# Attention inside a three-stage kernel: the key chunks of a half in two parts of four units instead of four parts of two

## What is computed

```python
q, k, v = (proj(Wq), proj(Wk), proj(Wv))
dots = jnp.einsum('bhqd,bhkd->bhqk', q, k) * scale
attn = jax.nn.softmax(dots, axis=-1)
out = jnp.einsum('bhqk,bhkd->bhqd', attn, v)
out = out.transpose(0, 2, 1, 3).reshape(b, n, INNER)
out = jnp.einsum('bne,ce->bnc', out, Wo)
return out + x
```

## Time and profile before

| | |
|---|---|
| median of 3 runs | 408.19 us (408.17 to 408.68) |
| profiled execution, its own time | 409.11 us |
| its span | 407.2 us |
| TensorE busy | 395.0 us, 97% |
| VectorE busy | 224.5 us, 55% |
| ScalarE busy | 254.7 us, 63% |
| GpSimd busy | 292.7 us, 72% |

### The profile page before, as it was taken

One profiled execution on the slowest core, in us unless ns is written; L12 is line 12 of the kernel. 1 busy time (PEld: TensorE's weight loads), 2 busy tenths in 40 slices (PEclk: granted clock), 3 DMA queues, 4 the chain that ended last, 5 costly groups with the idle time before them and its releaser, 6 DMA issues.

```text
span 407.2 us, 6494 instructions
## 1 busy us (share of the span) xinstructions
PE 395.0 (97%) x2518; PEld 238.1 (58%) x2518; DVE 224.5 (55%) x304; ACT 254.7 (63%) x347; POOL 292.7 (72%) x145
## 2 busy tenths in 40 slices
PE   8898999999999999999999999999999989999996
PEld 8765554454555445544645555464558535489995
DVE  1798765565656555656665565657563700564322
ACT  1556566676667575767676575858573596436763
POOL 3062088969899989999998999899989487900011
PEclk9999999999999999999999999999999999999999
DMA  7000101011220121012103222240125014000001
GB/s 247 2 1 0 54 0 54 6 47 26 82 52 2 54 54 52 3 54 54 52 2 105 48 110 54 54 150 7 57 52 157 0 55 155 2 1 14 15 26 53
DMA packets 28507, 20.49 MB, mean 50 GB/s; under 512 B 21276, under 2 KB 23708, under 8 KB 28476
## 3 DMA queue, kind: packets, MB, share of 16 engines
q1 hardware_dynamic: 27900, 19.09, 17.3%
q10 hardware_dynamic: 576, 0.98, 0.7%
HBM read 18.77 MB, written 1.17 MB: 49 GB/s over the span
## 4 chain that ended last, share of the span: by engine, by line
PE 88%; DVE 4%; ACT 2%; DMA 2%; SPq 1%; issue 1%; POOL 0%; ACTq 0%; POOLq 0%
PE acc_o L583 27%; PE slot L571 24%; PE slot L509 9%; PE slot L497 6%; PE slot L518 4%; PE acc_o L639 4%; PE slot L628 4%; PE acc_o L476 2%; PE acc_o L436 2%; DVE half_maxes L961 2%; PE slot L594 2%; DMA max_plane<-rows_scratch 1%; SPq L386 1%; PE slot L451 1%; PE slot L534 1%; PE acc_o L451 1%
## 5 line engine op out<-in xcount | busy, mean ns | idle before, releaser
L961 DVE TENSOR_REDUCE half_maxes<-slot 128x2 f32<-128x1024 f32 x128 | 156.3, 1225 | 98.1 <-PE slot L509 97.9
L761 ACT ACTIVATE probs<-slot 128x1024 f32<-128x1024 f32 x128 | 124.7, 1024 | 82.2 <-PE slot L571 82.2
L583 PE MATMUL acc_o<-probs,v_all 128*64 128x512 f32 x512 | 123.7, 604 | 0.0
L1160 POOL TENSOR_TENSOR sums<-sums,probs 128x1024 f32<-128x1024 f32 x31 | 74.0, 2387 | 2.4 <-ACT probs L761 2.3
L1160 POOL TENSOR_TENSOR odd_sum<-odd_sum,probs 128x1024 f32<-128x1024 f32 x31 | 74.5, 2404 | 0.0
L1160 POOL TENSOR_TENSOR sums<-probs 128x1024 f32<-128x1024 f32 x16 | 37.9, 2368 | 44.0 <-ACT probs L761 44.0
L583 PEld LDWEIGHTS acc_o<-probs,v_all 128*64 128x64 f32 x512 | 31.2, 136 | 59.0 <-issue 39.7
L509 PE MATMUL slot<-k_round,q_round 64*128 64x512 f32 x256 | 56.9, 447 | 1.6 <-DVE half_maxes L961 1.3
L509 PEld LDWEIGHTS slot<-k_round,q_round 64*128 64x128 f32 x256 | 23.6, 183 | 57.0 <-issue 46.3
L571 PE MATMUL slot<-q_round,k_round 64*128 64x512 f32 x256 | 51.8, 400 | 1.7 <-ACT slot L819 0.8
L571 PE MATMUL slot<-q_round,k_rest 64*128 64x512 f32 x256 | 50.6, 390 | 0.0
(11 more groups left out here) (114 smaller groups left out, 423.1 us busy)
## 6 DMA issues: line engine op xcount, KB each, us to landing
max_plane<-rows_scratch SPq DMA_DIRECT2D x16, 512.0 KB, 3.6
inv_sb<-inv_scratch SPq DMA_DIRECT2D x14, 256.0 KB, 3.9
max_rows_of<-maxes SPq DMA_DIRECT2D x128, 0.5 KB, 2.0
v_all<-in_fc SPq DMA_DIRECT2D x4, 512.0 KB, 5.9
fc_late<-in_fc SPq DMA_DIRECT2D x4, 512.0 KB, 5.6
residual<-in_x SPq DMA_DIRECT2D x2, 512.0 KB, 5.9
out_h<-probs SPq DMA_DIRECT2D x8, 128.0 KB, 1.8
v_all<-in_w ACTq DMA_DIRECT2D x3, 256.0 KB, 7.4
```

The source lines that it names most:

```text
L583: last = pe.matmul(acc_o[head_rows(h), cols], v_all[:, s, kc, head_rows(h)], probs[unit(s, kc, half) % TILES][:, h, :], start=(kc == 0), s ...
L761: act.activation(probs[u % TILES][:, :, :].rearrange("p h n -> p (h n)"), slot[:, :], ACT.Exp, scale=SCALE).then_inc(exped, 1)
L961: dve.reduce_max(half_maxes[:, :, qc, keys], slot[:, :].rearrange("p (h n) -> p h n", h=2), AX.X).then_inc(maxed, 1)
L1160: pool.tensor_tensor(chain[:, :, :], first[:, :, :], probs[kc][:, :, :], ALU.add).then_inc(own, 1)
```

## The change

A half has two parts of four units instead of four parts of two. A part is now max, exp, exp, max, exp, max, exp, max, then what stands beside, the fills, and the values of the four units of the part before: sixteen matmul instructions in a row. Written ahead are kc 4 of both halves and kc 5 of the second half (22 units in all, 44 before). The den, inv and ffn items and the norms are put at the ends of the new parts.

```diff
--- before.py
+++ after.py
@@ -43,7 +43,9 @@
 BANK = 512
 SLOTS = 3
 UNITS = 2 * KCH
-PARTS = KCH
+PARTS_OF_HALF = ((0, 1, 2, 3), (4, 5, 6, 7))
+HALF_PARTS = len(PARTS_OF_HALF)
+PARTS = 2 * HALF_PARTS
 TILES = KCH
 CONV_BANK = (0, 1, 6, 7)
 
@@ -68,16 +70,22 @@
 EXP_TABLE_BEHIND = ("max", *MAXES[6])
 
 
-FFN_ITEMS = {(STEPS - 1, 0): [("wo",)], (STEPS - 1, 3): [("nt",)], (STEPS - 1, 5): [("xa",)], (STEPS - 1, 6): [("last den", 0)]}
-
-
-PREFILLED = (2, 4, 6)
-UNFILLED = ((0, 2, 0), (STEPS - 1, 4, 0), (STEPS - 1, 4, 1))
+FFN_ITEMS = {(STEPS - 1, 0): [("wo",)], (STEPS - 1, 2): [("nt",), ("xa",)], (STEPS - 1, 3): [("last den", 0)]}
+
+
+PREFILLED = (4, 5)
+UNFILLED = ((STEPS - 1, 4, 0), (STEPS - 1, 5, 0)) + tuple((s, 5, 0) for s in range(STEPS))
 
 
 def units_of(s, part):
 
-    return [(s, 2 * (part % 4) + i, part // 4) for i in range(2)]
+    return [(s, kc, part // HALF_PARTS) for kc in PARTS_OF_HALF[part % HALF_PARTS]]
+
+
+def maxes_of(s, part):
+
+    first = AHEAD + s * UNITS + sum(len(units_of(s, p)) for p in range(part))
+    return [("max", *m) for m in MAXES[first:first + len(units_of(s, part))]]
 
 
 def beside_values(s, part):
@@ -85,28 +93,29 @@
     items = []
     if part == 0 and s + 1 < STEPS:
         items += [("k", s + 1), ("q", s + 1)]
-    if part == 3 and s > 0:
+    if part == 1 and s > 0:
         items.append(("den", s - 1))
     return items + FFN_ITEMS.get((s, part), [])
 
 
 def part_items(s, part):
 
-    maxes = [("max", *m) for m in MAXES[AHEAD + 2 * (s * PARTS + part):][:2]]
-    items = maxes[:1]
-    items += [("exp", *u) for u in units_of(s, part)] + maxes[1:]
+    maxes, exps = maxes_of(s, part), [("exp", *u) for u in units_of(s, part)]
+    items = maxes[:1] + exps[:2] + maxes[1:2]
+    for e, m in zip(exps[2:], maxes[2:] or [None] * len(exps[2:])):
+        items += [e, m] if m else [e]
     beside = beside_values(s, part)
     items += beside
-    if part % 4 < 3:
-        items.append(("fill", *units_of(s, part + 1)[0]))
+    if part % HALF_PARTS + 1 < HALF_PARTS:
+        items += [("fill", *u) for u in units_of(s, part + 1)]
     if s > 0 or part > 0:
         items += [("pv", *u) for u in units_of(*divmod(s * PARTS + part - 1, PARTS))]
     if part == 0 and s > 0:
         items.append(("o", s - 1, 1))
-    if part == 4:
+    if part == HALF_PARTS:
         items += [("o", s, 0)] * (s + 1 < STEPS) + [("inv", s - 1)] * (s > 0)
-    if s == STEPS - 1 and part in (1, 2, 3):
-        items.append(("norms", part))
+    if s == STEPS - 1 and part in (0, 1):
+        items += [("norms", 1)] if part == 0 else [("norms", 2), ("norms", 3)]
     return items
 
 
```

## The result

The changed kernel takes 421.51 us (419.42 to 421.75), the kernel before, run beside it, 408.33 us (408.17 to 408.68). The ratio of the means is 1.031, with a 95% interval of 1.0277 to 1.0344: 13.2 us slower. The forecast was 423 us in a range of 411 to 430, with 0.88 on slower.

What follows compares the result with a forecast made beforehand. TensorE's instruction stream, plus losses at turns from scores to values, was taken as the bound. Terms -11.5 + 5.0 + 14.2 + 2.5 + 4.65 = +14.9 us, added to 408.19, gave 423 us, range 411 to 430.

Steps and rivals of the forecast that it cites:

- Turns: TensorE's switches from scores to values and back: 32 fewer at 0.36 us each, -11.5 us.
- Max terms: 22 more max-term matmul pairs on TensorE, as fewer slots are written ahead, 0.23 us each: +5.0 us.
- Chained waits: Steps 1 to 6: items wait for the slot of the item three before; 2.37 us a steady step, +14.2 us.
- E4: Fifth of a part's eight items, a score unit (E; row-max items are M, numbering from 0): 0.25 us late.
- E6: Seventh of a part's eight items, a score unit: 0.19 us late, waiting for a row-max drain.
- First step: Waits of 3.0 us around a written-ahead unit, 1.24 for parts 2 and 3, against 1.8 before: +2.5 us.
- Last step: Waits behind norms, roots and transpose: 7.3 us against 2.65 before, +4.65 us.
- three waits over 2 us: Sign that the forecast is right: three TensorE waits of over 2 us in the last step.
- Rival 1: Drains are no limit, score items keep up; only -11.5 and +5.0 count: some 402 us; chance 0.08.
- Rival 2: Only E4's 0.25 us wait exists in parts; first and last step lose half: 412 us; chance 0.10.
- Rival 3: GpSimd's lumped adds make the denominators wait, one 2.4 us add in each of seven steps: 440 us; chance 0.06.
- Rival 4: New waits halve TensorE's clock for one part in eight, 4 parts of some 8 us: 455 us; chance 0.03.

Runs made afterwards that it cites:

- short_both: Changed kernel with row-max reading half of each head's columns and exp covering one head from the ninth unit on: 402.49 us, 0.9844 to 0.9873 of before.
- short_exp: Changed kernel with ScalarE's exp covering only the first head's 512 columns from the ninth unit on: 417.80 us, 1.0214 to 1.0248 of before.
- no_table: Changed kernel with the two roots of the last step's first layernorm replaced by exponentials, so no table change: 418.48 us, 1.0224 to 1.0263 of before.
- hybrid: Changed kernel in steps 0 to 6, with the last step in the order of before: 417.84 us, 1.0191 to 1.0258 of before.
- last_step_a: Kernel before with only its last step reordered, output projection behind the first two maxes, longer values runs, one written slot: 409.02 us, 0.9993 to 1.0034 of before.

## Why the prediction was right, and where its terms were off

- **Turns (-11.5).** Right. The runs of sixteen save 0.16 us each in the trace (3.58 against twice 1.87). The other 0.20 can't be read from the changed kernel, in which those places are gone, but with short drains a step is 0.77 us less, the sum of four turns at 0.36 and three max terms; taken by itself a turn is (0.77 + 0.69) / 4 = 0.365. By the rule of the Trainium skill (TensorE: Matmul & The Clock Gate, The mechanism) that weight loads overlap matmuls only in another row group, it would be an estimated 0.33.
- **Max terms (+5.0).** 0.23 each, right (0.70 for three). Their net cost was less: 2.6 us alone, since the first step and the stretch from the output projection on came out 1.4 us shorter.
- **Chained waits (+14.2).** The mechanism, the items and their sizes are as worked out: E4 0.26 late (0.25), E6 0.18 (0.19), M5 on time, and M7, which had 0.05 in my sum, on time as well. All waits of a steady step come to 2.25 us where I had 2.65, and before it was 0.13 where I had 0.28. Most of the error is at the key projection and the denominators, 0.20 and 0.21 in my sum: both start 0.39 behind M7, and even without any wait they start 0.32 behind it (short_both, short_exp), since they are a turn themselves. So 0.07 us of each is a wait, and I had counted the price of the turn again. Net, a step was 1.35 us longer, not 1.62. The prediction's first paragraph names one place of a steady step in which before waits for a slot; its list of waits has a second of the same size, at the denominators (L594, six times, 1.9 us).
- **First step (+2.5).** From the first score unit to the second key projection I had four turns, two terms, this 2.5 (its parts add up to 2.44) and the next step's part 0: -1.44 + 0.46 + 2.5 + 0.45 = +1.97 us. Measured: +2.75 - 1.08 = +1.67.
- **Last step (+4.65).** Its three waits are where I put them, 2.15, 1.5 and 1.9 us against 2.1, 2.3 and 2.2, so the sign of three waits over 2 us came for the first alone. Behind the output projection I had -1.44 + 0.46 + 6.6 - 2.65 = +2.97 us, and the stretch grew by 2.85; but 1.6 of these are the clock's, so the net waits came to 2.2 instead of 3.95. Of the 1.7 too much, 1.05 is in these three (the second, behind the norms, and the third, behind the transpose, were costed too high); the other 0.7 I did not place.
- **Rivals.** Rival 1 fails on the waits; with short drains it holds in the steady steps, but not for the whole. Rival 2 (E4's wait alone) fails on E6. Rival 3: GpSimd's work stayed at 35.3 us in a step, and no wait of TensorE for it appeared. Rival 4, the clock, did come, but as one stretch of 3.4 us instead of four parts: 1.6 us, which no term of mine held.

Put together, my terms came to 1.97, 9.97 (six steps up to the output projection) and 2.97 us, and the stretches measured 1.67, 8.1 and 2.85. The forecast is 1.5 us above the median by two errors of opposite sign: waits too large by some 3.9 us, and no 1.6 us for the clock. That the number came so near is in part luck; without the fall of the clock it would have been some 3 us off, still inside the range.

## What to carry to other kernels

Before putting more work between two changes of shape, lay out how a slot turns round (the item's own writes, the drain, the release) against TensorE's work for that item and the two that follow it. Where the first is longer, the item three places on is late: here 2.30 us against 2.05 for E M E. Where two engines drain the slots in turn, as here, speeding up one moved the wait to the other, so try both together; an experiment that leaves out half of each drain does it cheaply. And ask of each piece of work that is added or taken away which waits it changes: a price taken from TensorE's instructions alone was 5.0 us where the kernel paid 2.6.

## What the runs showed of the hardware

TensorE's granted clock fell to its lower level behind some waits: behind one of 2.15 us in the changed kernel, from 335.3 to 338.7; behind 1.23 and 1.80 us with 2.2 us of work between them (no_table); behind 1.20 and 0.37 us in the first step (hybrid, where it cost 1.4 us). The length of the wait does not decide it. The clock stayed full behind 2.01 us in the profiled execution of last_step_a, behind 1.19 and 0.38 us in the first step of the changed kernel, and behind 0.94 and 1.11 us in before.

It isn't the same in each execution either. The changed kernel's mean clocks were 0.996, 0.990, 1.000 and 0.991, and the execution at 1.000 was the shortest, 419.42 us against 421.47 to 421.75; one of 17 executions of before had 0.995. So the changed kernel lost some 2 us in three of four executions. Only one of these three has a profile, and there the place is known: 1.6 us on top of the wait of 2.15. What decides between two executions with the same waits no run shows. The Trainium skill (TensorE: Matmul & The Clock Gate, What's actually happening) says that the chip sets TensorE's clock by how busy it has been recently; the rows agree in that every fall that I located stands behind waits.
